# Outputs of a gated recurrence moved to GpSimd, the product kept in PSUM, and the stage around it laid out anew

## The reference

```
# 1. gated linear attention, 16 heads, key dim 8, value dim 16
q, k, v = x@Wq, x@Wk, x@Wv
gk = log_sigmoid(x@Wgk1@Wgk2 + bgk2) / 16
h_t = h_{t-1} * exp(gk_t)[..., None] + k_t[..., None] * v_t[..., None, :]
o_t = einsum('bhk,bhkv->bhv', q_t * 8**-0.5, h_t)
o = rmsnorm(o) * gnw * silu(x@Wg);  x = layernorm(x + o@Wo)
# 2. cross attention: every token has 64 indices into 64 context rows
ckv = ctx @ W_kv_down.T;  kv = ckv[indices] @ W_kv_up.T
x = layernorm(x + softmax(q.k) v @ W_out.T)
# 3. causal attention and a mixture of 8 experts (top 2)
```

## Time and profile before

| | us |
|---|---|
| median of 3 runs | 1363.28 (1363.03 to 1363.65) |
| the profiled execution | 1363.14 |
| its span in the profile | 1361.4 |
| PE, DVE, ACT, POOL busy in the span | 1283.8, 973.9, 642.8, 140.5 |

### The profile page before, as it was taken

One profiled execution on the slowest core, in us unless ns is written; L12 is line 12 of the kernel. 1 busy time (PEld: TensorE's weight loads), 2 busy tenths in 40 slices (PEclk: granted clock), 3 DMA queues, 4 the chain that ended last, 5 costly groups with the idle time before them and its releaser, 6 DMA issues.

```text
span 1361.4 us, 19541 instructions
## 1 busy us (share of the span) xinstructions
PE 1283.8 (94%) x7802; PEld 953.8 (70%) x7802; DVE 973.9 (72%) x1481; ACT 642.8 (47%) x942; POOL 140.5 (10%) x225
## 2 busy tenths in 40 slices
PE   8787768999899999999999999999999999999997
PEld 6354436677655555558888788888888888888886
DVE  7899997787798998848676655655646556555566
ACT  5687764346468877874332432323323223233233
POOL 5000003000523423310000000000000000000000
PEclk9898889999999999999999999999999999999999
DMA  5000001004602221203000011201101102010001
GB/s 140 1 1 1 0 1 36 2 1 147 209 27 67 64 56 51 68 20 109 17 1 17 16 58 43 70 16 39 47 8 47 39 17 70 16 39 16 0 16 47
DMA packets 40332, 55.82 MB, mean 41 GB/s; under 512 B 9553, under 2 KB 26625, under 8 KB 40241
## 3 DMA queue, kind: packets, MB, share of 16 engines
q1 hardware_dynamic: 35056, 43.67, 10.5%
q0 software_dynamic: 3648, 10.09, 2.6%
q10 hardware_dynamic: 1536, 0.81, 0.2%
HBM read 43.73 MB, written 10.55 MB: 40 GB/s over the span
## 4 chain that ended last, share of the span: by engine, by line
PE 52%; DVE 2%; ACT 0%; issue 0%; ACTq 0%; DVEq 0%
PE PS L2513 25%; PE PS L2526 24%; PE PS L2276 1%; PE PS L114 0%; PE PS L2539 0%; PE PS L2257 0%; PE PS L2290 0%; DVE OT_all L2674 0%; DVE r_st L2352 0%; DVE r_on L2369 0%; DVE r_on L2349 0%; PE PS L2551 0%; DVE X L2361 0%; DVE x_mid L2665 0%; ACT X L2635 0%
## 5 line engine op out<-in xcount | busy, mean ns | idle before, releaser
L2596 ACT ACTIVATE x_g<-PS,x_bias 128x512 f32<-128x512 f32 x256 | 175.9, 687 | 493.4 <-PE PS L2513 493.3
L2513 PE MATMUL PS<-x_h,x_w 128*128 128x512 f32 x1536 | 398.7, 395 | 0.0
L2526 PE MATMUL PS<-x_mid,x_w 128*128 128x512 f32 x1488 | 383.9, 393 | 1.1 <-DVE x_w L2248 1.1
L2513 PEld LDWEIGHTS PS<-x_h,x_w 128*128 128x128 f32 x1536 | 286.1, 188 | 64.7
L2526 PEld LDWEIGHTS PS<-x_mid,x_w 128*128 128x128 f32 x1488 | 279.2, 188 | 65.7 <-DVE x_w L2248 1.6
L2665 DVE CAST x_mid<-x_g 128x512 fp32r<-128x512 f32 x256 | 109.2, 427 | 267.3 <-ACT x_g L2596 266.9
L2115 DVE TENSOR_REDUCE a_M<-PS 128x2 f32<-128x1024 f32 (+1 forms) x144 | 173.1, 1223 | 24.5 <-PE PS L1812 18.2
L2667 DVE TENSOR_TENSOR x_mid<-x_g,x_mid 128x512 fp32r<-128x512 f32 x256 | 177.3, 693 | 8.8
L2053 ACT ACTIVATE f_parts<-PS 128x512 f32<-128x512 f32 x224 | 120.8, 601 | 36.2 <-PE PS L1866 24.8
L1889 PE MATMUL PS<-f_parts,aV 128*32 128x256 f32 (+1 forms) x960 | 75.1, 394 | 0.2 <-POOL f_parts L1700 0.2
L696 ACT ACTIVATE c_hot<-c_idxT,c_cid 128x1024 bf16<-128x1024 bf16 x65 | 70.6, 1138 | 5.2 <-PE PS L337 3.9
(11 more groups left out here) (385 smaller groups left out, 1577.9 us busy)
## 6 DMA issues: line engine op xcount, KB each, us to landing
x_raw<-L_ffn_e_w SPq DMA_DIRECT2D x32, 512.0 KB, 3.8
...
```

The costliest lines, as they stand in the source:

```text
L2513: last = e.matmul(PS[:, f % 2, :], w1[n % 2][u][:, kt, f * P:(f + 1) * P], self.rows(v, k)[:, kt, :], start=m == 0 and kt == 0, stop=m == ...
L2526: last = e.matmul(PS[:, 2 + 2 * (it % 2) + d, :], w2[n % 2][v][:, f, d * P:(d + 1) * P], mid[u][:, f % RM, :], start=f == 0 and m == 0, st ...
L2596: e.activation(g[s % RG][:, :], PS[:, f % 2, :], ACT.Gelu, bias=b1[:, n, f:f + 1]).then_inc(A.sem, 1)
```

## The change

1. The output of steps 0 to 30 moves to GpSimd (`output` is now a helper that both engines call); VectorE keeps only that of step 31.
2. The product is written in place into PSUM, and the scan reads it there and writes to qh. The ring has 7 slots; the scan, not the product, waits for `sums`, and `values(jj)` waits for scan jj - 2.
3. `sums`, OT's copies, `turn` and `tokens` signal and wait by halves of 512 columns.
4. Of each four sign tiles GpSimd makes one (`indicator`, a comparison that gives 0 or 1; `winb` and `fix` correct for the other coding); ScalarE makes 48, and the 65th is GpSimd's too.
5. Kblk (`keys`) is made by GpSimd from a copy in SBUF; the normed rows of the first two blocks by GpSimd from a copy in X (`out_stored` on ScalarE, `out_rows_pool`), and their statistics are read from X.
6. All cases of the loop stand in other slots, on every engine. X's second half is turned in banks 6 and 7, counts begin at slot 5.

```diff
-        RQ, RS = 6, 6
+        RQ, RS = 7, 6
+            self.og[m] = (KT[:, 0:T] if m else z[:, :]).rearrange(...)
+        of_scalar = [n for n in range(NCTX) if n % 4 < 3]
+        taken = list(itertools.accumulate((2, 2, 1, 0, 0, 2, 2, 1, ...)))
+        def output(e, jj):
+            e.wait_ge(s_h, jj + 1)
+            ...
+            e.tensor_tensor(qh[:, jj % RQ, :], qh[:, jj % RQ, :], QT[:, batch(jj // HD)], ALU.mult).then_inc(s_qh, 1)
# GpSimd
+                def indicator(u):
+                    if u:
+                        e.wait_ge(s_cnt, min(u, 15))
+                    n = 4 * u + 3 if u < 16 else NCTX
+                    e.tensor_scalar(hot[:, n % RS, :], self.idxT[:, :], float(3 * 16 + u), None, ALU.is_ge).then_inc(s_hot, 1)
+                def keys(b, g):
+                    e.tensor_tensor(Kblk[:, b, g, :, :], kT[...], self.m16[...], ALU.mult).then_inc(s_kblk, 1)
+                e.wait_ge(A.sem, A.at("idx"))
+                indicator(0)
+                for jj in range(NJ - 1):
+                    output(e, jj)
+                    for u in range(1, 16):
+                        if jj == (5, 6, 8, 12, 14, 16, 18, 20, 23, 24, 26, 27, 28, 29, 30)[u - 1]:
+                            indicator(u)
+                    if jj in (22, 23, 24, 25):
+                        ...
+                        keys((jj - 22) // KD, (jj - 22) % KD)
+                    elif jj == 28:
+                        self.out_rows_pool(e, 0, s_row)
+                indicator(16)
+                self.out_rows_pool(e, 1, s_row)
# TensorE
-                        e.wait_ge(s_kv, jj - 1)
+                        e.wait_ge(s_h, jj - 1)
                 def turn(q):
-                    e.wait_ge(s_o, q + 1)
+                    for half in range(2):
+                        e.wait_ge(s_o, 2 * q + half + 1)
...
# VectorE
-                    if jj >= RQ:
-                        e.wait_ge(s_s, (jj - RQ) // 4 + 1)
-                    e.tensor_tensor(qh[:, jj % RQ, :], wide(2 * (jj % 2)), KT[:, batch(jj // HD)], ALU.mult).then_inc(s_kv, 1)
+                    e.tensor_tensor(wide(2 * (jj % 2)), wide(2 * (jj % 2)), KT[:, batch(jj // HD)], ALU.mult).then_inc(s_kv, 1)
...
+                    if jj >= RQ:
+                        e.wait_ge(s_s, 2 * ((jj - RQ) // 4) + 2)
+                    e.tensor_tensor_scan(qh[:, jj % RQ, :], decay[:, batch(jj // HD)], wide(2 * (jj % 2)), 0.0, ALU.mult, ALU.add).then_inc(s_h, 1)
                 for jj in range(NJ):
                     state(jj)
-                    if jj == 2:
+                    if jj + 1 < NJ:
+                        product(jj + 1)
+                    else:
+                        output(e, jj)
+                    if jj == 3:
                         parts_lo(1)
+                        x_lo(2, 6)
...
# ScalarE
+                def turned_out(q):
+                    for half in range(2):
+                        sums_out(q, half)
+                    for half in range(2):
+                        tokens(q, half)
...
+    def out_stored(self, e, m, banks):
+        e.wait_ge(self.OS[m].sem, self.OS[m].at("wo"))
+        e.activation(self.X[:, m * TB:(m + 1) * TB, :], self.pair_banks(banks[0]), ACT.Copy).then_inc(self.OA[m].sem, 1)
+    def out_rows_pool(self, e, m, done):
+        e.wait_ge(self.OV[m].sem, self.OV[m].at("nmr"))
+        for t in range(TB):
+            x = self.X[:, m * TB + t, :]
+            last = e.tensor_scalar(x, x, self.o_rstd[m % 2][:, t:t + 1], self.o_nmr[m % 2][:, t:t + 1], ALU.mult, ALU.add)
+        last.then_inc(done, 1)
```

388 lines of the change are left out of this document (207 added, 181 removed).

## The result

The changed kernel took 1355.96 us (median of 5 runs, 1352.63 to 1359.11) against 1363.28 beside it (1362.08 to 1365.45): ratio 0.9944, 95% interval 0.9923 to 0.9964. It is faster, clear of the noise, by 7 us where 35 were forecast, and the time lies outside the range of 1320 to 1345. Its runs spread more than those of before.

What follows compares the result with a forecast made beforehand. VectorE, busy 160.3 of 168.1 us from first scan to last, was taken to set the pace: 1363.1 - 35.0 (outputs) + 2.7 (scan behind product) - 2.5 (Kblk) = 1328.3 us, with waits kept and tail 0; range 1320 to 1345.

Steps and rivals of the forecast that it cites:

- Outputs off VectorE: VectorE's queue, first to last scan: 31 output instructions go, each with its pitch of 1.13 us: -35.0 us.
- the scan behind its product: VectorE: with no output between product and scan, their pitch is 1.26 instead of 1.12; 19 steps x 0.14 = +2.7 us.
- the product in place: VectorE: writing the product into PSUM and scanning from there costs zero; upper end 33 us.
- floor of 125.7: VectorE's time from first scan to last after the change, without waits, in us; a new step is 3.46.
- rival 2: VectorE's five loop instructions with two SBUF inputs wait for GpSimd: 6.5 us, 1335, at most 1341; chance 0.2.
- Waits kept: VectorE's waits between first and last scan stay at the 7.3 us of before; ends 0 and about 20.
- GpSimd's load: GpSimd in the stage: outputs 2.5 us each, 17 indicators 1.17 each, keys and rows; 106 us within 125.7.
- Tail "0": Behind the last scan: same instructions; last indicators, copies and counts fit into 4.8 us before the counts' turn: 0 added.
- TensorE's clock, 0.93 to 1: TensorE's granted clock, 0.89 before, was expected to rise to 0.93 to 1 with less idleness in each step.
- Rival 1: TensorE and ScalarE set the stage's pace: 141.6 us against 133, +8.7, 1337, up to 1345; chance 0.2.
- Rival 4: VectorE's product written in place into PSUM costs a second pass of the data: +33 us, 1361; chance 0.05.
- Rival 3: GpSimd's output can't run beside VectorE's scan: a step is 4.78 us against 4.45, total 1383; chance 0.05.

Runs made afterwards that it cites:

- Number 5: Changed kernel with the outputs back on VectorE, all else kept: 1370.07 us, ratio 1.0065 to the kernel before.
- number 7: Changed kernel with ScalarE's low-rank copy ahead of the two signs in slot 6: 1350.99 us, ratio 0.9928 to the kernel before.
- number 2: Changed kernel with GpSimd's 17 indicators replaced by memsets of a constant: 1349.01 us, ratio 0.9916 to the kernel before.
- number 3: Changed kernel with a multiplication by one added behind each indicator's comparison, 3.63 us each: 1362.44 us, ratio 1.0007 to the kernel before.
- number 10: Changed kernel with the last two indicators on VectorE, unit 14's a slot earlier, ScalarE's last signs ahead of the seventh group's copies: 1349.28 us, ratio 0.9915.
- number 12: Changed kernel with low-rank copy, fourth output gate, second square root and counts' unit 2 reordered, last two indicators on VectorE, last signs earlier: 1342.40 us, ratio 0.9863.
- number 6: Changed kernel with the product kept in SBUF, so the scan has two SBUF inputs, and `sums` awaited by the product: 1378.70 us, ratio 1.0127.

## Why the prediction was wrong

Forecast 1328.3, profiled 1352.6: 24.3 us. By its own steps:

- *Outputs off VectorE (-35.0), the scan behind its product (+2.7), Kblk (-2.5), the product in place (0):* right. Undisturbed scans come 3.44 to 3.47 apart (3.46 forecast). The stage without its waits is 145.2 - 14.8 = 130.4 against a floor of 125.7, and 4.6 of that are the stretched instructions of rival 2, so the floor was right within 0.1.
- *"Waits kept": 7.3:* this is the step that failed in the stage; in the same measure it was 14.8, +7.5. It took the size of the waits from the row of before, while the step between them went from 4.45 to 3.46. Number 5 shows the link: with the old step the same orders have 6.6 us of waits. What I ran through by slots was TensorE's amount of work in slots 12 to 17. It gave one stall of 0.6, and VectorE waited 3.7 there (0.6 for sums, 0.3 and 2.8 for values). What stalls isn't an amount of work, it is a pause for ScalarE's copy or an indicator, with or without matmuls at the low level behind it (4.36 at 58, which number 7 removed with one line; 2.81 at 99, behind a pause of 1.75 for ScalarE's silu, after which the gate's 24 matmuls took 3.14, as fast as elsewhere). No wait of ScalarE for the counts was in my sum at all, and there were 11.4 us of them ahead of its signs (5.2 before).
- *GpSimd's load:* the output was right (2.5, measured 2.415), the indicator was wrong (1.17, measured 2.768), taken from a row of another operation. In the stage that cost nothing (number 2), though the margin ends somewhere below 3.63 (number 3). In the tail it is 3.2 us.
- *Tail "0":* the other step that failed, and the larger one: +10.4, and 0.3 of that was in the sum for rstd and nmr, so +10.1. Its reason was "the counts' turn arrives at 199.81, 4.8 after its end, and the last indicators, copies and counts fit into that". That is when the turn came in the old order; when the last signs and indicators come in the new one I did not work out. In the trace of before ScalarE's last sign ended 1.2 us behind the last scan's start (193.98 against 192.74), in that of after 6.7 (176.77 against 170.04), and the last indicator 11.3 (181.35). The turn came 15.2 us behind the scan's end in place of 4.8. Number 5 shows that this tail comes without the moved outputs too (24.0), so it belongs to the new order and the indicators on GpSimd; number 10 took away 4.6 of it, number 12 5.4. The low clock has a part in it too: TensorE is busy 2.4 us longer in the tail.
- *TensorE's clock, 0.93 to 1:* 0.93 in the stage, at the very edge; 0.73 in the tail.
- *Rival 2* was right in kind and nearly in size: 4.6 us against 6.5, in three of the five instructions that it counted and in the 128x4 one, which it had not. *Rival 1*, at 1337, was right in kind, as the waits are for TensorE and ScalarE, but that its +8.7 is near the 7.5 is partly luck: it took TensorE as busy for 126 us with 15.6 of idleness, and measured were 120.3 and 24.9. Its upper end was also added up wrong: 126 + 5.6 + 21 - 133 is 19.6, which makes 1348 and not 1345. *Rival 4* is excluded by products of 1.213. *Rival 3* is excluded by scans of 2.28 beside outputs of 2.42; number 6 shows it at work, at a smaller price, for a scan that reads both inputs from SBUF.

The sum comes out with them: 1328.3 + 7.5 (waits) + 4.6 (rival 2) + 10.1 (tail) = 1350.5, and what is left is in the start and the rest of the program (+0.2, +1.8). I had given each rival its chance as if only one could happen, and the range ended where rival 1 alone ended. They don't exclude each other: they add. The tail was nobody's rival. Nor did my signs of being wrong cover it: VectorE idled 15.9 us in the loop, not over 20, and an output took 2.42, not over 3.4.

Shown by experiments: the price of the indicator and where it counts, that VectorE's two-input instructions are stretched beside GpSimd's reads, that the waits rise with the shorter step, the hand-off at 58, and that the tail comes of the order and the indicators. Shown by single traces: what the halves are worth. Not settled: how the added 7.5 us of waits divide between order and low clock, since the low level came in different places, and behind some pauses only; nor why the runs of the changed kernel and of number 12 spread over 6.5 and 7.8 us (4 or 5 runs each), where the kernel before has 3.4 to 5.5 (5 to 19 runs).
